# Pair products of a recommendation model: four samples a matmul, diagonal evictions, and a VectorE block transpose for the TensorE row transposes

## The reference

```python
sparse_embed = emb_tables[field_idx[None, :], x_sparse]        # (B, 26, 64)
z = sparse_embed.reshape(B, N_FIELDS * K)                      # 1664 values
gram = jnp.einsum('bik,bjk->bij', sparse_embed, sparse_embed)
iu, ju = jnp.triu_indices(N_FIELDS, k=1)
inner = gram[:, iu, ju]                                        # 325 values
dnn_in = jnp.concatenate([x_dense, z, inner], axis=-1)         # HID = 2002
h = jax.nn.relu(dnn_in @ w1 + b1)
out = jax.nn.sigmoid(h @ w2 + b2)
```

## Time and profile before

| | |
|---|---|
| runs | 517.21, 516.97, 516.66 us, median 516.97 |
| profiled execution | span 516.5 us from the first to the last instruction; no time of its own beside the span is listed |
| TensorE (PE) | busy 494.6 us, 96% of the span |
| VectorE (DVE), ScalarE (ACT) | 297.6 us (58%), 242.9 us (47%) |
| GpSimd (POOL) | 237.0 us, nothing after about 307 us |
| TensorE clock granted, mean | 0.951 of full speed |
| DMA | 78.40 MB, 152 GB/s |

### The profile page before, as it was taken

The page is one execution under the profiler, slowest core; times in us unless marked ns, Lnnn a source line. Parts: engine busy times, 40 slices in busy tenths (PEclk is TensorE's granted clock), DMA queues, the critical chain, the costliest instruction groups (busy, mean ns, idle before and its releaser), DMA issues.

```text
span 516.5 us, 7944 instructions
## 1 busy us (share of the span) xinstructions
PE 494.6 (96%) x3089; PEld 423.2 (82%) x3089; DVE 297.6 (58%) x619; ACT 242.9 (47%) x358; POOL 237.0 (46%) x215
## 2 busy tenths in 40 slices
PE   8668999799999999999999999999999999999996
PEld 8457888788888888888888888888888888888885
DVE  2365568549525883489448763775586455436422
ACT  2455547439313763286337632772475343334311
POOL 5777777778778887777767750000000000000000
PEclk9797679699988999999999999999999989999998
DMA  6987548645745665467646753453256327665500
GB/s 158 252 253 188 109 104 219 173 82 140 206 105 132 179 191 165 104 168 191 176 101 158 234 139 114 134 185 113 81 160 195 111 81 243 182 195 170 169 11 0
DMA packets 28757, 78.40 MB, mean 152 GB/s; under 512 B 7696, under 2 KB 7704, under 8 KB 28720
## 3 DMA queue, kind: packets, MB, share of 16 engines
q1 hardware_dynamic: 22064, 71.07, 44.0%
q0 software_dynamic: 6656, 6.83, 11.4%
HBM read 77.87 MB, written 0.00 MB: 151 GB/s over the span
## 4 chain that ended last, share of the span: by engine, by line
PE 86%; POOL 4%; DMA 3%; DVE 2%; issue 2%; ACT 2%; ACTq 0%
PE acc L358 22%; PE acc L359 22%; PE acc L342 21%; PE side L300 12%; PE side L310 5%; POOL z L256 4%; PE side L288 2%; DMA w_raw<-in_L_rec_w_dram 1%; PE side L281 1%; DMA z<-in_L_rec_emb_tables_dram,idx 1%; ACT w_hi L393 1%; DVE w_lo L468 1%; DMA idx<-in_r_x_sparse_dram 1%; PE side L319 1%; DVE tail L507 0%
## 5 line engine op out<-in xcount | busy, mean ns | idle before, releaser
L256 POOL DMA_INDIRECT z<-in_L_rec_emb_tables_dram,idx x208 | 236.1, 1135 | 68.3 <-issue 62.5
L358 PE MATMUL acc<-w_hi,x_hi 128*128 128x502 f32 (+3 forms) x512 | 211.0, 412 | 1.4 <-ACT x_hi L398 1.3
L359 PE MATMUL acc<-w_lo,x_hi 128*128 128x502 f32 (+3 forms) x512 | 204.6, 400 | 0.0
L468 DVE TENSOR_TENSOR w_lo<-w_raw,w_hi 128x1002 fp32r<-128x1002 f32 (+1 forms) x139 | 165.3, 1208 | 48.0 <-ACT w_hi L393 47.5
L393 ACT CAST w_hi<-w_raw 128x1002 fp32r<-128x1002 f32 (+1 forms) x139 | 141.8, 1039 | 52.7 <-PE acc L342 44.8
L342 PE MATMUL acc<-w_hi,x_lo 128*128 128x502 f32 (+3 forms) x512 | 146.2, 397 | 0.0
L358 PEld LDWEIGHTS acc<-w_hi,x_hi 128*128 128x128 f32 (+1 forms) x512 | 100.6, 196 | 21.3 <-issue 2.1
L342 PEld LDWEIGHTS acc<-w_hi,x_lo 128*128 128x128 f32 (+1 forms) x512 | 99.2, 194 | 20.5
L359 PEld LDWEIGHTS acc<-w_lo,x_hi 128*128 128x128 f32 (+1 forms) x512 | 100.0, 195 | 18.3
L300 PEld LDWEIGHTS side<-pair_v,pair_u 128*26 128x26 f32 x1024 | 66.9, 168 | 7.3 <-issue 3.8
L300 PE MATMUL side<-pair_v,pair_u 128*26 128x26 f32 x1024 | 66.5, 212 | 3.7 <-DVE pair_v L489 3.5
(11 more groups left out here) (34 smaller groups left out, 160.0 us busy)
## 6 DMA issues: line engine op xcount, KB each, us to landing
w_raw<-in_L_rec_w_dram SPq DMA_DIRECT2D x131, 501.0 KB
z<-in_L_rec_emb_tables_dram,idx POOLq DMA_INDIRECT x208, 3.7
w_raw<-in_L_rec_w_dram SPq DMA_DIRECT2D x8, 270.1 KB
w2b<-in_L_rec_w_dram SPq DMA_DIRECT2D x1, 501.0 KB, 7.2
w2b<-in_L_rec_w_dram SPq DMA_DIRECT2D x1, 500.0 KB, 8.2
w_raw<-in_L_rec_w_dram SPq DMA_DIRECT2D x8, 50.9 KB
w_raw<-in_L_rec_b_dram SPq DMA_DIRECT2D x8, 3.9 KB
idx<-in_r_x_sparse_dram SPq DMA_DIRECT2D x1, 104.0 KB, 2.9
```

The costliest lines, as they stand in the source:

```text
L256: pool.indirect_dma_start(out=z[:, t % 2, K * f:K * (f + 1)], out_offset=None, in_=emb_rows, in_offset=bass.IndirectOffsetOnAxis(ap=idx[:, ...
L358: nc.tensor.matmul(o, hi, wh, start=k == 0, stop=False)
L359: nc.tensor.matmul(o, hi, wl, start=False, stop=False)
L468: nc.vector.tensor_tensor(w_lo[0:rows, slot, :], w_raw[0:rows, m % RAW, :], w_hi[0:rows, slot, :], ALU.subtract).then_inc(w_lo_done, 1)
```

## The change

- G: one matmul now takes four samples, `b`, `b+32`, `b+64` and `b+96`. `pair_u` is laid out as four blocks of 32 fields (26 and 6 of padding, zeroed once) so the stationary operand has 128 columns; the moving operand has 4 × 26 = 104 columns. Of the 128 × 104 results only the four diagonal blocks are wanted. A bank holds 4 matmuls (16 samples, as before); a tile has 32 matmuls in 8 banks in place of 128.
- A bank's reader makes four copies of 32 partitions × 104 values, one for each quarter of the partitions, in place of one of 26 × 416.
- R on TensorE and ScalarE is gone. At the place of R, VectorE transposes `gram` in blocks of 32 × 32 into `square`, and then adds as before. The bank rotation has two uses a tile fewer.
- `pair_u` is written with runs of 32 values in place of runs of 128.
- `PLAN`, `WARM`, T, O, X and the wide layer are as before.

```diff
-    GB = 16
-    GBANKS = P // GB
+    QUAD = 32
+    SIDES = 4
+    APART = P // SIDES
+    GB = 4
+    GBANKS = APART // GB
...
+    def placed(q, s):
+        quad = (APART * s + GB * q) // QUAD
+        m0 = GB * q % QUAD
+        return slice(QUAD * quad, QUAD * (quad + 1)), slice(m0, m0 + GB)
...
-        pair_u = sb("pair_u", [P, FIELDS, P], f32r)
+        pair_u = sb("pair_u", [P, SIDES, QUAD, APART], f32r)
-        gram = sb("gram", [FIELDS, P, FIELDS], fp32)
-        square = sb("square", [P, FIELDS, FIELDS], fp32)
+        gram = sb("gram", [P, QUAD, FIELDS], fp32)
+        square = sb("square", [P, FIELDS, QUAD], fp32)
...
                 for g in range(GB):
-                    s = GB * q + g
-                    last = nc.tensor.matmul(bank(("G", t, q))[0:FIELDS, g * FIELDS:(g + 1) * FIELDS],
-                                            pair_u[:, :, s], pair_v[:, :, s], start=True, stop=True)
+                    b = GB * q + g
+                    last = nc.tensor.matmul(
+                        bank(("G", t, q))[0:SIDES * QUAD, wide * g:wide * (g + 1)],
+                        pair_u[:, :, :, b].rearrange("p s f -> p (s f)"),
+                        pair_v[:, :, b:P:APART].rearrange("p f s -> p s f"), start=True, stop=True)
...
-            def product_rows(t):
-                pe.wait_ge(gram_act, gram_counts(GBANKS * (t + 1))[0])
-                pe.wait_ge(gram_dve, gram_counts(GBANKS * (t + 1))[1])
-                for j in range(2):
-                    bank_free(("R", t, 0), j)
-                    for i in range(RR):
-                        last = nc.tensor.transpose(
-                            bank(("R", t, 0), j)[:, FIELDS * i:FIELDS * (i + 1)],
-                            gram[:, :, RR * j + i], ident[0:FIELDS, 0:FIELDS])
-                    last.then_inc(rows_made, 1)
...
-                    last = nc.scalar.copy(pair_u[0:K, f, :], high)
+                    last = nc.scalar.copy(pair_u[0:K, :, f, :].rearrange("p s f b -> p f s b"),
+                                          high.rearrange("p f (s b) -> p f s b", s=SIDES))
...
-                    nc.vector.tensor_copy(gram[:, GB * q:GB * (q + 1), :].rearrange("i b j -> i (b j)"),
-                                          bank(("G", t, q))[0:FIELDS, 0:GB * FIELDS]).then_inc(gram_dve, 1)
+                    for s in range(SIDES):
+                        of = bank(("G", t, q))[QUAD * s:QUAD * (s + 1), 0:SIDES * FIELDS * GB]
+                        rows, at = placed(q, s)
+                        last = nc.vector.tensor_copy(
+                            gram[rows, at, :],
+                            of.rearrange("p (m j) -> p m j", m=GB)[:, :, FIELDS * s:FIELDS * (s + 1)])
+                    last.then_inc(gram_dve, 1)
...
-                dve.wait_ge(rows_done, 2 * t + 1)
+                dve.wait_ge(gram_act, gram_counts(GBANKS * (t + 1))[0])
+                dve.wait_ge(gram_dve, gram_counts(GBANKS * (t + 1))[1])
+                nc.vector.transpose(square[:], gram[:].rearrange("p m j -> p j m")).then_inc(turned, 1)
                 nc.vector.tensor_copy(tail[:, PAIRS:PAIRS + DENSE], dense[:, t, :])
-                dve.wait_ge(rows_done, 2 * t + 2)
+                dve.wait_ge(turned, t + 1)
```

More of the change, by code:

```diff
@@ L51, in product_interaction_mlp_kernel @@
     XS = 4
-    RR = FIELDS // 2
     STEPS = HALVES * TILES // GROUP
@@ L101, in count, with bank @@
         return sum(e[0] in kinds for e in ORDER[:ORDER.index(event) + 1])
-    USES = [(*e, j) for e in ORDER if e[0] != "O" for j in range(2 if e[0] == "R" else 1)]
+    USES = [e for e in ORDER if e[0] not in "OR"]
     BANKS = 4
-    def bank(event, j=0):
-        return side[USES.index((*event, j)) % BANKS]
+    def bank(event):
+        return side[USES.index(event) % BANKS]
+    def placed(q, s):
+        quad = (APART * s + GB * q) // QUAD
+        m0 = GB * q % QUAD
+        return slice(QUAD * quad, QUAD * (quad + 1)), slice(m0, m0 + GB)
     emb_rows = emb.rearrange("f v k -> (f v) k")
@@ L170, in product_interaction_mlp_kernel @@
         gram_dve = sem("gram_dve")
-        rows_made = sem("rows_made")
-        rows_done = sem("rows_done")
+        pad_zero = sem("pad_zero")
+        turned = sem("turned")
         tail_done = sem("tail_done")
@@ L263, in _, with bank_free @@
         def _(pe):
-            def bank_free(event, j=0):
-                u = USES.index((*event, j))
+            def bank_free(event):
+                u = USES.index(event)
                 if u >= BANKS:
[L268 to L271, removed]
+                    kind, t, q = USES[u - BANKS]
+                    if kind == "G" and q % 2 == 0:
                         pe.wait_ge(gram_act, gram_counts(GBANKS * t + q + 1)[0])
@@ L294, in pair_products @@
                 if q == 0:
+                    if t == 0:
+                        pe.wait_ge(pad_zero, 1)
                     pe.wait_ge(pairs_act, len(BATCHES) * (t + 1))
@@ L297, in pair_products @@
                 bank_free(("G", t, q))
+                wide = SIDES * FIELDS
                 for g in range(GB):
-                    s = GB * q + g
-                    last = nc.tensor.matmul(bank(("G", t, q))[0:FIELDS, g * FIELDS:(g + 1) * FIELDS],
-                                            pair_u[:, :, s], pair_v[:, :, s], start=True, stop=True)
-                last.then_inc(gram_made, 1)
-            def product_rows(t):
-                pe.wait_ge(gram_act, gram_counts(GBANKS * (t + 1))[0])
-                pe.wait_ge(gram_dve, gram_counts(GBANKS * (t + 1))[1])
-                for j in range(2):
-                    bank_free(("R", t, 0), j)
-                    for i in range(RR):
-                        last = nc.tensor.transpose(
-                            bank(("R", t, 0), j)[:, FIELDS * i:FIELDS * (i + 1)],
-                            gram[:, :, RR * j + i], ident[0:FIELDS, 0:FIELDS])
-                    last.then_inc(rows_made, 1)
+                    b = GB * q + g
[3 more added lines that the diff above has]
+                        pair_v[:, :, b:P:APART].rearrange("p f s -> p s f"), start=True, stop=True)
+                last.then_inc(gram_made, 1)
             def transpose_tail(t):
@@ L414, in read_pairs @@
                 if q % 2 == 0:
+                    if q == 0 and t >= 1:
+                        act.wait_ge(turned, t)
                     act.wait_ge(gram_made, GBANKS * t + q + 1)
[L416 to L423, removed]
+                    for s in range(SIDES):
+                        of = bank(("G", t, q))[QUAD * s:QUAD * (s + 1), 0:SIDES * FIELDS * GB]
+                        rows, at = placed(q, s)
+                        last = nc.scalar.copy(
+                            gram[rows, at, :],
+                            of.rearrange("p (m j) -> p m j", m=GB)[:, :, FIELDS * s:FIELDS * (s + 1)])
+                    last.then_inc(gram_act, 1)
             def high_tail(t):
@@ L462, in _ @@
             nc.vector.memset(w2b[:, 1, 0:2], 0.0).then_inc(w2_zero, 1)
+            nc.vector.memset(pair_u[:, :, FIELDS:QUAD, :].bitcast(fp32), 0.0).then_inc(pad_zero, 1)
             def split_piece(m):
@@ L487, in pair_operands @@
                     part = slice(K * par, K * (par + 1))
-                    nc.vector.tensor_copy(pair_u[K:2 * K, f, :], x_lo[part, t % XS, first:first + n, :])
+                    low = x_lo[part, t % XS, first:first + n, :]
+                    nc.vector.tensor_copy(pair_u[K:2 * K, :, f, :].rearrange("p s f b -> p f s b"),
+                                          low.rearrange("p f (s b) -> p f s b", s=SIDES))
                     last = nc.vector.tensor_copy(pair_v[K:2 * K, f, :],
@@ L494, in read_pairs @@
                 if q % 2 == 1:
+                    if q == 1 and t >= 1:
+                        dve.wait_ge(turned, t)
                     dve.wait_ge(gram_made, GBANKS * t + q + 1)
-                    nc.vector.tensor_copy(gram[:, GB * q:GB * (q + 1), :].rearrange("i b j -> i (b j)"),
-                                          bank(("G", t, q))[0:FIELDS, 0:GB * FIELDS]).then_inc(gram_dve, 1)
+                    for s in range(SIDES):
+                        of = bank(("G", t, q))[QUAD * s:QUAD * (s + 1), 0:SIDES * FIELDS * GB]
+                        rows, at = placed(q, s)
+                        last = nc.vector.tensor_copy(
+                            gram[rows, at, :],
+                            of.rearrange("p (m j) -> p m j", m=GB)[:, :, FIELDS * s:FIELDS * (s + 1)])
+                    last.then_inc(gram_dve, 1)
             def make_tail(t):
```

4 lines of the change are left out of this document (2 added, 2 removed).

## The result

The changed kernel takes 492.2 us (median of 4 runs, 491.6 to 494.3) beside 517.09 for the kernel before in the same runs; the ratio is 0.9508, 95% interval 0.9466 to 0.9550. The forecast was 467, range 455 to 485: faster was right, the size was wrong by 25 us, and the measured time lies outside the range. Of the 50 us forecast, 25 came.

The account below looks back on a forecast made before the run. TensorE, busy 96% of the span, was taken as the bound. Span 516.5 − 42.6 (products and R, tiles 2 to 7) − 5.1 (clock) − 5.5 (start) + 3.3 (waits at X) = 466.6 us; median 467, range 455 to 485.

Parts of the forecast that it names:

- the load of 128 columns sets about 119 ns: G's new pair matmul on TensorE: priced like R's transposes, 3.8 us a tile in place of 7.8, saving 4.0.
- 61 ns is not array time but the pace of the instructions: Old pair products on TensorE: 61 ns taken as instruction pace, the lower bound for a new pair matmul.
- as much as a wide one: Rival for G: a matmul of 104 columns costs 227 ns, 21 us more, 488 us; chance 0.08.
- my half-clock argument: Pair products: 60 ns at clock 0.50 too, so at most 1.4 cycles a column; 232 columns 135 ns at full clock.
- R: TensorE's 26 row transposes a tile go: 3.1 us a tile saved.
- The clock: TensorE's three half-clock stretches of 3.4 us counted as won back: 5.1 us, bounds nothing to 5.1.
- The start: Tiles 0 and 1: gathers hold tile 2's fourth T at 117.9 instead of 123.35; gain 5.5 us, bounds 3 and 6.1.
- The chain to X: Evictions, weight split, VectorE transpose, additions: TensorE waits 1.1 us at X of tiles 4, 6 and 7, +3.3 us.
- the transpose: VectorE's block transpose of 128 × 832 values in the way to X: 1.04 us, bounds 0.6 and 2.1.
- the wait of 0.3 us: VectorE's weight split ahead of X: ends at E+2.9, not E+2.6, waiting for ScalarE's half; E ends the last product.
- The 81 ns of the Trainium skill: Page's sustained spacing for a weight load and a 128-column matmul: a tile's products would take 2.6 us.
- The 0.93 us of the Trainium skill: Page's price for four VectorE reads of a PSUM bank, 120 cycles plus one a value, against 1.13 us from the rows.

Follow-up runs that it names:

- run_u: Changed kernel with the stationary operand's 128 columns in one run: 119 ns a pair matmul; 586 us beside 629 for the kernel before.
- change_third: The changed kernel once more, unaltered, where the kernel before takes 522.1 us: 492.4 us, ratio 0.943.
- change_late: Changed kernel with X of tiles 0, 4, 6 and 7 one turn later, nothing else: 490.0 us, ratio to the kernel before 0.940.
- run_u_late_again: Changed kernel with stationary columns in one run and X of tiles 0, 4, 6, 7 one turn later: 466.0 us, ratio to before 0.895.
- run_all_late: Changed kernel with stationary columns in one run, later X, and gram laid out for VectorE's transpose to read one run: 464.6 us, ratio to before 0.890.
- run_uv: Changed kernel with stationary and moving columns both in one run: 104 ns a matmul in most places; 555 us beside 624 for the kernel before.
- rows_back: Changed kernel with 26 unused TensorE transposes a tile put back at R's place: 67 ns each; 585 us beside 626 for the kernel before, inconclusive.
- before_run: Kernel before with each sample's 26 stationary columns in one run: 32 ns a product, not 61; 620 us beside 626, not read.

## Why the prediction was wrong

**The step that failed** is "the load of 128 columns sets about 119 ns", with its lower bound "61 ns is not array time but the pace of the instructions". The change takes about 236 to 256 ns: 7.6 us a tile, against the 3.8 that I took and the 7.8 before. Over six tiles 22.8 us of the 25 are this one term. What sets the price is the read of the stationary columns with a step: in one run the same matmul takes 119 ns. Two readings went into the miss. I took R's transposes as the nearest row because both load 128 columns with a step; but they load them on 26 partitions and as plain fp32, and move 26 columns, and the change loads on 128 partitions and as fp32r, and moves 104. Which of these makes R's 119 ns out of 250 was not tried. And I read "60 ns at either clock" as a sign that neither operand counted, where it meant that the read of a stepped operand, which has a pace of its own, counted. Had I divided 61 ns by 26 columns (2.3 ns) and multiplied by 128 or by 104, I would have had 300 or 244 ns. The rival "as much as a wide one", 227 ns with 0.08, was near the truth in number, and my half-clock argument against it was the error. That it was near is luck: it was put there for fewer columns costing as much as many, which `run_u` shows to be wrong.

The trace of before also held a warning that I passed over: the "keep warm" matmuls, 128 stationary and 128 moving columns, both in one run. In the chain, ten of them at half clock and 16 at full clock:

```profile
41.51 2.13 PE side L281 x10
112.39 1.78 PE side L281 x16
```

They take 213 and 111 ns. That is 0.43 ns for each of their 256 columns at full clock, and it doubles at half clock; the old pair products, with stepped operands, took 1.2 ns for each of their 52 columns at either clock. This does not refute a pace of instructions by itself, but it is a second price for a column, and the layout is what sets the two rows apart beside the size and the type (fp32 here, fp32r there).

**R**: right. It was 3.1 us a tile on TensorE's list and is gone: 18.5 us over six tiles, nearly all of the 19.5 that the part behind tile 2's fourth T gained.

**The clock**: mis-sized. 5.1 us forecast, 1.7 came: two of the low stretches were left where there were three. As the products still take as long, the same long runs of them stand in the list. The count varies between executions: behind tile 2's T change_third has one low stretch and change_late one, run_u_late_again and run_all_late, with products half as long, have none. So 1.7 us is one trace's figure, and 3.4 would have been another's.

**The start**: right that gathers hold it, and near in size, T at 116.55 against 117.9, gain 6.8 against 5.5; but the way there was not the one forecast. 6.3 us were gained already at tile 1's G (87.27 against 93.60, where 3.46 us of idle are gone), and as its products took 8.2 us and not 3.8, TensorE came to tile 2's second T, at about 101, without a wait. The figure is also loose: change_third, the same kernel, has its fourth T at 119.08. The faster products of run_u_late_again hardly moved it: there the T before it waits 2.30 us for gathers, and the fourth stands at 115.89:

```profile
109.89 0.66 PE L297 MATMUL side<-ident,z 128*128 128x128 f32 x4 [2.30 <-DMA z<-in_L_rec_emb_tables_dram,idx]
115.89 0.38 PE L297 MATMUL side<-ident,z 128*128 128x128 f32 x2
```

**The chain to X**: right in place and sum, 3.0 us of idle against 3.3 (tile 0's X, which the forecast did not name, waits 1.78 us too, in the start). Inside it the transpose was mis-sized, 1.83 us and not 1.04, near my upper bound; the weight split came without the wait of 0.3 us that I gave it, and the whole chain took 6.5 us from the start of the evictions at 242.61 to 249.14, where I had 6.5 as well (E+0.2 to E+6.7): the smaller terms made up for the larger one, and that the sum fits is luck. VectorE in order of time at tile 4 (start us, us):

```profile
242.61 1.09 DVE L509 COPY gram<-side 32x104 f32<-32x104 f32 x4 [2.34 <-PE side L312]
243.73 1.20 DVE L474 TENSOR_TENSOR w_lo<-w_raw,w_hi 128x1002 fp32r<-128x1002 f32 x1
244.85 1.86 DVE L520 STREAM_TRANSPOSE square<-gram 128x832 f32<-128x832 f32 x1
246.61 0.14 DVE L521 COPY tail<-dense 128x13 f32<-128x13 f32 x1
246.74 2.40 DVE L524 TENSOR_TENSOR tail<-square 128x25 f32<-128x25 f32 x25
```

**The two figures from pages.** The 81 ns of the Trainium skill ("TensorE: Matmul & The Clock Gate", section "Back-to-back issue gap") was met by no pair products here: 104 ns is the least measured, with both operands in a run. The 0.93 us of the Trainium skill ("VectorE: DVE Perf Modes", section on the TRN2 errata) for four VectorE reads of PSUM, an estimate from its table, stands against 4 × 262 = 1.05 us measured; my 1.13 from the rows before is a little nearer. What that section says of a fixed extra latency is said of operations that read SBUF; for reads of PSUM its table has the 120 cycles and one a value.

**The sum.** Behind tile 2's fourth T: products 6 × 0.2, R 18.5, clock 1.7, X −3.0 makes 18.4 of 19.5 us; 1.1 us is not attributed. The device time stands 1.8 us above the span of the same execution in every run that has both, not 0.5: the 0.5 most likely came from holding the span of one execution of before, 516.5, against the median of others.

## What to carry to other kernels

Price a matmul of few columns by its stationary operand, by column and by how the columns lie: here a matmul with 128 of them cost 0.9 ns a column in one run at full clock and about 1.9 with a step at either clock, and a quarter of the matmuls took the same time. Packing four samples into one matmul gave next to nothing until the columns lay in a run; then it gave 23 us, with the scattered writes moved to engines that had time. And before a short duration is called a floor, divide it by each operand's columns.

## What the runs showed of the hardware that was not expected

- A matmul of few columns whose stationary operand has a step of 104 to 512 bytes takes about twice as long as one with it in a run, at full clock: 26 columns of fp32r 61 and 32 ns (step 512 bytes), 128 columns 250 and 116 ns (128 bytes), fp32 transposes on 26 partitions 119 and 67 ns (104 bytes; the least clean of the three pairs, as the operands differ in more than the step).
- With a step of 128 bytes the pace is the same at half clock: 18 in 4 us at 91 to 95 us. In one run it follows the clock: two banks 0.95 us at full and 1.92 at half clock in run_u.
- With both operands in one run the price is near that of all columns, stationary and moving together, at one a cycle: 256 columns (L281 of before) 111 ns, and 213 at half clock; 232 (run_uv) 104 ns; 154 (rows_back) 67 ns. An estimate from 2.4 and 1.2 GHz gives 107, 213, 97 and 64. That load and move add up was not tested by itself, and 26 + 26 columns in before_run (the moving ones with a step) take 32 ns against 22 by that estimate.
- VectorE's block transpose of 128 × 832 fp32 values: 1037 ns from one run, 1834 ns from a step of 104 bytes.
- 104 values into `gram` cost VectorE 262 ns in a run and 343 ns with a step of 128 bytes, ScalarE 239 and 329 ns; ScalarE's copy of 512 values into `pair_u` 604 and 1104 ns.
